# One scale per matrix, W2's norm as a trace on TensorE, three units' butterflies on the DVE, and banks named in TensorE's order

## The reference

```python
i, f, g = x @ Wi.T, x @ Wf.T, x @ Wg.T
gate = sigmoid(f);  v = silu(i) * (1 - gate)
o[t] = gate[t] * o[t-1] + v[t]                   # along the rows of a batch
o = o * rsqrt(mean(o * o) + eps) * gnorm_w * g * sigmoid(g)
y = o @ Wo.T
```

```python
hidden = silu(x @ W1.T) * (x @ W3.T)             # 2048 wide
hidden = fwht(hidden)                            # butterflies over 2048, times 1/sqrt(2048)
out = hidden @ W2.T
```

## Time and profile before

| | us |
|---|---|
| median of 3 runs | 787.03 |
| profiled execution | 789.14 |
| its span, first to last instruction | 786.3 |
| TensorE matmul busy | 729.9 (93%) |
| DVE busy | 378.6 (48%) |
| ACT busy | 255.4 (32%) |
| POOL busy | 250.2 (32%) |
| mean granted TensorE clock, of full speed | 0.972 |

### The profile page before, as it was taken

One profiled execution on the slowest core, in us unless ns is written; L12 is line 12 of the kernel. 1 busy time (PEld: TensorE's weight loads), 2 busy tenths in 40 slices (PEclk: granted clock), 3 DMA queues, 4 the chain that ended last, 5 costly groups with the idle time before them and its releaser, 6 DMA issues.

```text
span 786.3 us, 8923 instructions
## 1 busy us (share of the span) xinstructions
PE 729.9 (93%) x3344; PEld 339.9 (43%) x3344; DVE 378.6 (48%) x700; ACT 255.4 (32%) x428; POOL 250.2 (32%) x240
## 2 busy tenths in 40 slices
PE   3298886999999999999999999999999999999993
PEld 2044443444444444444444444444444444444441
DVE  6888998883334357511333358322333364121114
ACT  5577754462223122312233123312232123121121
POOL 2937784221111253411112243310132234111114
PEclk9699997999999999999999999999999999999997
DMA  8904014000000012400000011500000013000002
GB/s 328 407 20 160 14 69 161 1 0 1 1 1 0 1 41 68 161 0 1 1 0 1 15 41 53 161 1 1 0 1 1 16 39 108 1 0 1 1 0 80
DMA packets 16026, 38.44 MB, mean 49 GB/s; under 512 B 1905, under 2 KB 2161, under 8 KB 15473
## 3 DMA queue, kind: packets, MB, share of 16 engines
q1 hardware_dynamic: 15984, 37.89, 13.8%
HBM read 29.49 MB, written 8.39 MB: 48 GB/s over the span
## 4 chain that ended last, share of the span: by engine, by line
PE 85%; DVE 7%; issue 3%; ACT 2%; DMA 1%; POOL 1%; DVEq 1%; SPq 0%; POOLq 0%; ACTq 0%
PE ps L417 27%; PE ps L418 27%; PE ps L419 27%; DVE ring L835 1%; PE ps L562 1%; PE ps L561 1%; DMA ring<-L_attn_Wf 1%; PE ps L461 1%; DVEq L790 1%; POOL hsp L1084 1%; DVE o_s L893 0%; DMA x1r<-x_rows 0%; DVE ab L924 0%; DVE sga L1004 0%; DVE si L888 0%
## 5 line engine op out<-in xcount | busy, mean ns | idle before, releaser
L417 PE MATMUL ps<-xb,ring 128*128 128x512 f16 x704 | 268.4, 381 | 9.5 <-DVE ring L835 4.9
L418 PE MATMUL ps<-xb,ring 128*128 128x512 f16 x704 | 268.3, 381 | 0.0
L419 PE MATMUL ps<-xb,ring 128*128 128x512 f16 x704 | 268.0, 381 | 0.0
L1084 POOL TENSOR_TENSOR hsp<-sga,hsp 128x512 f16<-128x512 f32 x64 | 75.5, 1179 | 250.8 <-ACT hsp L746 250.3
L997 DVE SCALAR_TENSOR_TENSOR sga<-ps,gate_c,sga 128x512 f32<-128x512 f32 x64 | 47.9, 748 | 140.3 <-ACT sga L736 140.3
L417 PEld LDWEIGHTS ps<-xb,ring 128*128 128x128 f16 x704 | 69.6, 99 | 93.9 <-issue 13.0
L419 PEld LDWEIGHTS ps<-xb,ring 128*128 128x128 f16 x704 | 69.2, 98 | 84.3 <-issue 1.9
L418 PEld LDWEIGHTS ps<-xb,ring 128*128 128x128 f16 x704 | 69.1, 98 | 84.0 <-issue 3.1
L417 PE MATMUL ps<-w2t,hsp 128*128 128x512 f16 x256 | 97.0, 379 | 3.3 <-POOL hsp L1084 2.9
L419 PE MATMUL ps<-w2t,hsp 128*128 128x512 f16 x256 | 97.0, 379 | 0.0
L418 PE MATMUL ps<-w2t,hsp 128*128 128x512 f16 x256 | 97.0, 379 | 0.0
(11 more groups left out here) (140 smaller groups left out, 747.9 us busy)
## 6 DMA issues: line engine op xcount, KB each, us to landing
ring<-W13t SPq DMA_DIRECT2D x16, 512.0 KB, 10.7
rows<-L_attn_hidden_states SPq DMA_DIRECT2D x16, 256.0 KB, 3.4
w2t<-W2t SPq DMA_DIRECT2D x8, 512.0 KB, 13.4
res<-L_attn_hidden_states SPq DMA_DIRECT2D x16, 256.0 KB, 4.0
x_rows<-res SPq DMA_DIRECT2D x16, 256.0 KB, 2.0
x1r<-x_rows SPq DMA_DIRECT2D x16, 256.0 KB, 3.3
out<-res SPq DMA_DIRECT2D x16, 256.0 KB, 3.6
ring<-L_attn_Wf SPq DMA_DIRECT2D x1, 1024.0 KB, 7.2
```

What stands on the lines that cost most here:

```text
L417: pe.matmul(dst, a_hi, b_hi, start=start, stop=False)
L418: pe.matmul(dst, a_hi, b_lo, start=False, stop=False)
L419: return pe.matmul(dst, a_lo, b_hi, start=False, stop=stop)
L1084: pool.tensor_tensor(hsp[:, c % 2, 1], sga[:, c % 2], hsp[:, c % 2, 0], ALU.subtract).then_inc(hid_lo, 1)
```

## The change

It has four parts.

1. *One power-of-two scale per matrix.* Wf, Wi and Wg are squared, summed and scaled in one piece each (AN.w.0), W1 and W3 have one scale each for all 16 pairs (one step WS.0.0 behind the last WN). The operations on scales become 128x1. GC is cut in three (GC, GD, GS): the maximum over the gain alone is taken without the scales, and only the last step uses them. HS goes; the bound for the hidden row comes in WS.0.0 from the exponents of the same matmul, and VS, later, makes the output's factor.
2. *W2's norm as a trace.* In place of the eight squares on ACT, TensorE multiplies the upper half (bf16) of each block of 128 columns of W2 by itself, 8 matmuls of 128 columns per unit, all 64 into one bank (W2N); the DVE masks the diagonal and sums it (W2D), W2S spreads the sum.
3. *Butterflies.* Units 2, 5 and 7 run on the DVE (FD), the other five on POOL. The scratch tiles are dealt anew, and so are the tiles for the squares.
4. *The tables.* All five orders are written anew, and TensorE's names the bank of each step behind a colon. From there on the first hidden chunks come before H2.7, GA and UP alternate with D otherwise, and the next batch's X1 to ZT lie at other chunks.

```diff
--- before.py
+++ after.py
...
-XT.0.0 AN.0.0 XT.0.1 AN.0.1 XT.0.2 AN.1.0 XT.0.3 AN.1.1 AN.2.0 AN.2.1 F.0.0 GC.0.0 I.0.0 G.0.0 W2S.0.0 I.0.1
...
+XT.0.0:4 XT.0.1:5 AN.0.0:6 XT.0.2:7 XT.0.3:0 AN.1.0:1 W2N.0.0:2 AN.2.0:3 W2N.1.0 W2N.2.0 F.0.0:4 W2N.3.0 W2N.4.0
+W2N.5.0 GC.0.0:6 I.0.0:5 W2N.6.0 W2N.7.0 G.0.0:7 W2S.0.0:1 I.0.1:0 F.0.1:3 G.0.1:4 AN.3.0:6 I.0.2:2 H2.0.0:5
...
+        ON_DVE = (2, 5, 7)
+        POOL_UNITS = (0, 1, 3, 4, 6)
...
-            spot = (4, 5, 6, 7, 0, 1, 2, 3)[turn % 8] if n < first_down else 4 + turn % 4
-            turn += 1
-            bank_of[step] = spot
-            if spot in last_on:
-                before[step] = last_on[spot]
-            last_on[spot] = step
+            if kind == "D" and t < TC:
+                if b > 0:
+                    before[step] = ("V", b - 1, t)
+                elif t in last_on:
+                    before[step] = last_on[t]
+            if ":" in word:
+                spot = int(word.split(":")[1])
+                bank_of[step] = spot
+                if spot in last_on:
+                    before[step] = last_on[spot]
+                last_on[spot] = step
...
+            def w2_products(m, _):
+
+                if m == 0:
+                    wait_bank("W2N", 0, 0)
+                pe.wait_ge(ld_w2[m], 16)
+                for j in range(8):
+                    last = pe.matmul(bank("W2N", 0, 0)[:, 0:P], unit_top(m)[:, chunk(j)], unit_top(m)[:, chunk(j)],
+                                     start=m == 0 and j == 0, stop=m == UNITS - 1 and j == 7)
+                last.then_inc(w2_gram, 1)
 
             def w2s(b, t):
                 wait_bank("W2S", b, t)
-                pe.wait_ge(squared, squares_to["W2N", UNITS - 1, 0])
-                pe.matmul(bank("W2S", b, t)[:, 0:UNITS], ones[:], w2n2[:], start=True, stop=True).then_inc(w2_norm, 1)
+                pe.wait_ge(w2_sum, 1)
+                pe.matmul(bank("W2S", b, t)[:, 0:1], ones[:], w2_part[:], start=True, stop=True).then_inc(w2_norm, 1)
...
-            def w2n(m, _):
-                act.wait_ge(ld_w2[m], 16)
-                if squares_to["W2N", m, 0] > 1:
-                    act.wait_ge(squared, squares_to["W2N", m, 0] - 1)
-                act.activation(junk[:], unit_raw(m).rearrange("p c d -> p (c d)"), ACT.Square,
-                               accum_out=w2n2[:, m:m + 1]).then_inc(squared, 1)
...
+            def attention_scales(w, _):
+                dve.wait_ge(aw_norm, w + 1)
+                src = bank("AN", w, 0)
+                dve.tensor_reduce(exps[:, 1:2], src[:, 0:2] if w == 3 else src[:], AX.X, ALU.add if w == 3 else ALU.max
+                                  ).then_inc(dve_chain, 1)
+                settle()
...
+            def gain_max(b, t):
+
+                dve.wait_ge(ld_gw, 16)
+                dve.tensor_scalar(neg_gw[:], gw[:], -1.0, None, ALU.mult).then_inc(dve_chain, 1)
+                dve.tensor_scalar(g_coef[:].bitcast(I32), gw[:].bitcast(I32), 0x7FFFFFFF, None, ALU.bitwise_and
                                   ).then_inc(dve_chain, 1)
                 settle()
+                settle()
+                dve.tensor_reduce(s_tmp[:, 5:6], g_coef[:], AX.X, ALU.max).then_inc(dve_chain, 1)
+                settle()
                 dve.wait_ge(ld_eye, 16)
+                dve.tensor_scalar(osq[:, 0:P], ident[:], s_tmp[:, 5:6], None, ALU.mult).then_inc(diag_rdy, 1)
...
+            def ws(b, t):
+                dve.wait_ge(w_norm, 1)
+                norms = bank("WS", b, t)[:, 0:2 * HC].rearrange("p (w c) -> p w c", w=2)
+                dve.tensor_reduce(w_sum[:], norms, AX.X, ALU.add).then_inc(dve_chain, 1)
+                dve.tensor_scalar(w_exp[:].bitcast(I32), norms.bitcast(I32), 24, None, ALU.logical_shift_right
+                                  ).then_inc(ws_read, 1)
+                settle()
+                for w in range(2):
+                    exponent_scales(w_sum[:, w:w + 1], dve_chain, w_s[:, w:w + 1], w13_inv[:, w:w + 1], w_srdy)
...
+            def w2_diagonal(b, t):
+                dve.wait_ge(w2_gram, UNITS)
+                dve.wait_ge(ld_eye, 16)
+                grid = bank("W2N", 0, 0)[:, 0:P]
+                dve.tensor_tensor(grid, grid, ident[:], ALU.mult).then_inc(dve_chain, 1)
+                settle()
+                dve.tensor_reduce(w2_part[:], grid, AX.X, ALU.add).then_inc(w2_sum, 1)
 
             def w2s(b, t):
                 dve.wait_ge(w2_norm, 1)
-                dve.tensor_reduce(s_tmp[:, 0:1], bank("W2S", b, t)[:, 0:UNITS], AX.X, ALU.add).then_inc(dve_chain, 1)
-                settle()
-                exponent_scales(s_tmp[:, 0:1], w2s_read, 1, w2_s[:], w2_inv[:], w2_srdy, less=5)
+                exponent_scales(bank("W2S", b, t)[:, 0:1], w2s_read, w2_s[:], w2_inv[:], w2_srdy, less=5)
+
+            def dve_butterfly(m, k):
+                n = ON_DVE.index(m)
+                if k == 0:
+                    dve.wait_ge(ld_w2[m], 16)
+                    if m > 2:
+                        dve.wait_ge(h2_mm, 2 * (unit_before(m) + 1))
+                elif k % 2 == 0:
+                    dve.wait_ge(w2_dve, 6 * n + k)
+                if k == 2:
+                    dve.wait_ge(w2_gram, m + 1)
+                to, a, b, op = butterfly(m, k)
+                dve.tensor_tensor(to, a, b, op).then_inc(w2_dve, 1)
```

More of the change, by code:

```diff
@@ L292, in steps_of @@
         def steps_of(text):
-            return [(kind, int(b), int(t)) for kind, b, t in (word.split(".") for word in text.split())]
+            return [(kind, int(b), int(t)) for kind, b, t in (word.split(":")[0].split(".") for word in text.split())]
         pe_steps, act_steps, dve_steps, pool_steps, sp_steps = (
@@ L478, in weight_norms, with spread_max @@
                     return
-                pe.wait_ge(aw_sq, 2 * w + p + 1)
+                pe.wait_ge(aw_sq, w + 1)
                 if w == 0:
                     pe.wait_ge(ones16_set, 1)
-                c0, c1 = PART[p]
                 for k in range(KC):
-                    last = pe.matmul(dst[:, 0:(c1 - c0) * P], ones16[:], squares[w][:, k, c0 * P:c1 * P],
-                                     start=k == 0, stop=k == KC - 1)
+                    last = pe.matmul(dst[:], ones16[:], squares[w][:, k * D:(k + 1) * D], start=k == 0, stop=k == KC - 1)
                 last.then_inc(aw_norm, 1)
-            def spread_max(kind, n):
-                wait_bank(kind, 0, 0)
-                pe.wait_ge(diag_rdy, n)
+            def spread_max(b, t):
+                wait_bank("GC", 0, 0)
+                pe.wait_ge(diag_rdy, 1)
                 pe.wait_ge(ones_set, 1)
-                pe.matmul(bank(kind, 0, 0)[:, 0:P], ones[:], diags[kind], start=True, stop=True).then_inc(diag_mm, 1)
+                pe.matmul(bank("GC", 0, 0)[:, 0:P], ones[:], osq[:, 0:P], start=True, stop=True).then_inc(diag_mm, 1)
             def project(kind, b, c, w, done):
@@ L643, in f @@
                     act.wait_ge(o_rdy, n - 1)
-                act.activation(gate[:, c % 2], bank("F", b, c)[:], ACT.Sigmoid, scale=unscale[:, 0, c:c + 1]
+                act.activation(gate[:, c % 2], bank("F", b, c)[:], ACT.Sigmoid, scale=unscale[:, 0:1]
                                ).then_inc(gate_rdy, 1)
@@ L653, in i @@
                     act.wait_ge(o_rdy, n)
-                act.activation(si[:], bank("I", b, c)[:], ACT.Sigmoid, scale=unscale[:, 1, c:c + 1]
+                act.activation(si[:], bank("I", b, c)[:], ACT.Sigmoid, scale=unscale[:, 1:2]
                                ).then_inc(sgi_rdy, 1)
@@ L675, in g @@
                     act.wait_ge(o_lo, n)
-                act.activation(sg[:], bank("G", b, c)[:], ACT.Sigmoid, scale=unscale[:, 2, c:c + 1]
+                act.activation(sg[:], bank("G", b, c)[:], ACT.Sigmoid, scale=unscale[:, 2:3]
                                ).then_inc(sgg_rdy, 1)
@@ L742, in up @@
                 if n == 0:
-                    act.wait_ge(h2_mm, 2 * UNITS)
+                    act.wait_ge(h2_mm, 14)
                 if n >= 2:
```

496 lines of the change are left out of this document (234 added, 262 removed).

## The result

The changed kernel takes 768.3 us (median of four runs, 766.9 to 770.3) against 787.0 of before: 0.976 of it, with a 95% interval of 0.974 to 0.979. With a second timing of five runs the median of all nine is 767.8. The prediction was 768.5, with a range of 757 to 782. The profiled execution of after was its longest run: 770.3, with a span of 768.5, against 789.14 and 786.3.

A forecast was written before the change was run, and what follows sets the result against it. Vector engines, above all the DVE, bound the first batch, TensorE's matmul columns the rest. GA.0.0 23.6 us earlier, less 3.4 for H2.7 and 1.7 for the clock, nets 18.5: 787.03 to 768.5 us, range 757 to 782.

The forecast's parts named there:

- The bound and where the gain is: Before GA.0.0 the vector engines bind, above all the DVE; behind it TensorE is full, so GA.0.0's shift is the gain.
- One scale per matrix, in the attention: Start of batch 0: fewer, narrower scale operations save some 9 us of DVE; GC at about 29.5, I.0.0 at 30.
- W2's norm: Ahead of GA.0.0: ACT loses 8.4 us of squares, TensorE gains 64 matmuls at 0.11 us each, bounds 6.4 to 17 in all.
- Butterflies: Ahead of GA.0.0: 18 operations move from POOL to the DVE, at a mean of 0.95 us, 0.68 to 1.65 each.
- Y.0.0 at 78: First output projection of batch 0 starts at 78 us, against 97.62 before; bounds 72 and 86.
- GA.0.0 at 110: The step from which TensorE is full starts at 110 us, against 133.6 before; bounds 103 and 120.
- H2.7 behind GA.0.0: Four H2.7 matmul pairs at 0.86 us now stand behind GA.0.0, which costs 3.4 us.
- The low clock, 1.7: Gaps ahead of GA.0.0 let TensorE's clock fall, which costs 1.7 us.
- Behind GA.0.0, 0 taken, bounds -4 and +6: Later batches: X1, V and W dealt in another way, nothing gained or lost on average; bounds -4 and +6 us.
- the DVE becomes the bound: Rival, ahead of GA.0.0: moved butterflies cost 1.65 us each, 12 on the path, 11.6 us lost, 780 us; chance 0.13.
- Weights late: Rival, ahead of GA.0.0: ACT's last square comes at 90 and not 82, Y chain 8 us later, 776.5 us; chance 0.13.
- the slower case: Rival, at the handovers: down projection's banks come free too late, up to 27.2 us of waiting, 795.7 us; chance 0.08.

The follow-up runs named there:

- less_dve_work: Kernel after without the second and third butterfly stage of W2's units 2 and 5, eight DVE operations left out: 766.0 us.
- wide_small_ops: Kernel after with the five small operations on each gate weight's scale made on 128x3 and not 128x1: 772.6 us.
- after_again: The kernel after, unchanged, timed and profiled a second time: 767.4 us.
- reordered: Kernel after with unit 2's butterflies on POOL and another order of the same steps from 60 us to GA.0.0 and at the last handover: 766.9 us.

## Why the prediction was right

- **The bound and where the gain is.** Right in the main: TensorE's work behind GA.0.0 is the same but for H2.7, and 17.2 us of the gain are the shift of GA.0.0. That the DVE's work counts in the prologue is borne out: DVE time put back came out at 0.7 to 0.9 of its size by the medians (8.6 us gave 6.2; the 5.3 us by which the operations on 128x3 are longer gave 4.8). Taken off, it gave less than half (less_dve_work), so now it is one bound of several.
- **One scale per matrix, in the attention.** Right in kind, too small in size. I put GC at 29.5 and I.0.0 at 30, with 28 as its lower bound; they are at 26.4 and 26.7. The waits of 6.45 and 4.87 us became 2.19 and none. The rule that the prediction quoted from the "GPSIMD Engine Reference" of the Trainium skill (section "1. Specifications") names two kinds of DVE instruction: those with two SBUF inputs, which I quoted, and those in a 2-port perf mode, which I left out. wide_small_ops has 1.1 against 0.17 us with one SBUF input, so the first kind alone does not cover it; whether these are of the second kind no run here shows.
- **W2's norm.** Too dear: 0.11 us per product predicted, 7 us in all, with 0.10 as the lower bound; measured 0.067, 4.3 us in all, below the bound. The 0.39 us of four products, from which I took 0.10, has the tail of the last one in it; 24 in a row take 1.54, so (1.54 - 0.39) / 20 = 0.058 us is what one more costs.

```profile
L567 PE MATMUL ps<-w2t 128*128 128x128 bf16 x64 | 4.3, 218 | 0.0
```

  By the rule on strided readers of "SBUF — State Buffer" of the Trainium skill (section "Door 1: The DMA port swizzle"), the trace agrees: every second bf16 costs nothing that shows. ACT's eight squares are worth 2.6 us at the end, of 6 at I.0.0.
- **Butterflies.** The mean on the DVE is 0.97 us (below; 0.88 in after_again), 0.95 was taken. Their use was not split between units: unit 2 is worth nothing, units 5 and 7 four us. POOL's unit 6, put at 103 to 107, ended at 110.1 (107.4 in after_again).

```profile
L1005 DVE TENSOR_TENSOR x1r<-w2t 128x512 f32<-128x512 f32 x12 | 11.4, 961 | 2.1 <-PE ps L588 2.1
L1005 DVE TENSOR_TENSOR w2t<-x1r 128x512 f32<-128x512 f32 x6 | 6.0, 1037 | 0.0
```

- **Y.0.0 at 78 (82.1; 79.7 in after_again).** The step that failed in the walk: I gave 69 us as the time when TensorE is through with its projections and let ACT's P.0.3 be last. In the trace unit 2 was last. H2.2.0 waited 3.54 us for the DVE's butterflies, and ACT's P.0.3 stood behind H2.2.0 in its order (75.98). TensorE then went without a gap from 71.61 to 82.12, at a clock of 0.57 from 72 on; at full clock these ten us would have been some four shorter (an estimate from that window). All this cost less than it seems: reordered removed it and GA.0.0 stayed.
- **GA.0.0 at 110 (116.5; 113.7 in after_again).** The largest miss, 3.7 to 6.5 us, still in the bounds of 103 to 120. Of it 1.7 to 4.1 us had come by Y.0.0. I let the stretch behind Y.0.0 be 32 us and it is 34: WS took the 3.6 us on the DVE that I gave it (90.36 to 94.0), but Y.0.2, Y.0.3 and all that follows stood behind it.
- **H2.7 behind GA.0.0**: 3.4 predicted, 3.4 measured. **The low clock, 1.7**: no term of its own. Behind GA.0.0 the clock is 0.99 before and after; the low stretches lie ahead of it, and their cost is in its start already. There it was larger than 1.7, as the 72 to 82 us above show.
- **Behind GA.0.0, 0 taken, bounds -4 and +6.** Measured -4.0: the bound itself. I read the wait of 2.9 us behind POOL and did not see that the trace gives another 1.5 us as busy time of transposes that stand in a row, part of it a wait for the DVE.

The sum by these terms: 23.6 - 3.4 - 1.7 + 0 = 18.5 predicted; 17.2 - 3.4 - 0 + 4.0 = 17.8 measured in the profile. Two misses of 4 and 6 us with opposite signs made it look more exact than its steps were: that the sum came within a microsecond is luck, while the mechanism and the range are not. Of the rivals, "the DVE becomes the bound" did not happen; it was one before and is one of several now. "Weights late" came in part: ACT's last square ended at 87.7, nearer to the 90 of that rival than to the 82 of the forecast, but nothing waited for it. WS was not waited for, and YN.0.0, behind the last square on ACT, waited another 1.9 us for the DVE (89.55). At the handovers, where the slower case would have shown, 1.43 us of waiting came and 4 us went.

## What to carry to other kernels

Walk the landmarks to the point behind which the bound engine is full, and price every edit as a shift of that point; then check the part behind it by its own rows, short stretches that look busy among them. When several engines are due at nearly the same time, the sum of single prices is not the price of all (17.7 against 9.3 us here): test by adding work to the suspected engine and by taking some off, at the same places if you can, since two different slopes (here 0.7 and 0.25 to 0.45, by different edits) speak for a balance and not for one bound. Profile the same kernel twice before you compare a landmark: one and the same program had GA.0.0 at 113.7 and 116.5. And an earlier start at a middle landmark (5.7 us at Y.0.0) may be worth nothing at the end.

## What the runs showed of the hardware

- A DVE operation on 128x3 with one SBUF source, 0.17 us with POOL idle, takes 1.05 to 1.14 beside POOL's butterflies in five of ten cases; on 128x1 it takes 0.15 in all.
- Two executions of the same program waited alike ahead of GC (2.19 and 2.18 us). In one the granted clock then was 0.50 from 26.7 to 29.7 us, in the other 1.00, and 0.57 from 36 to 40 us behind a wait of 2.75. A low clock ahead of a wait for another engine cost nothing at W2S (35.67 and 35.69); behind it, it did. They came out 2.8 us apart at GA.0.0.
- A 128x128 bf16 product with a new stationary operand each, both operands every second element, takes 0.067 us of busy time over 64 of them, and 0.058 us for one more in a row.
- A merged row of TensorE can have a wait in it: 16 transposes in a row, 2.25 us busy, held 0.36 us in which their weight loads stood still.
